# Gate and local input of a two-layer adaLN kernel: unrolled, three batches in flight, slots cleared inside the gate

## The reference, cut to what matters

```python
h = _layernorm(x) * (1 + ca) + sa
x = x + ga * attention(h)
h = _layernorm(x) * (1 + cb) + sb
x = x + gb * ffn(h)
```

## Time and profile before

| | us |
|---|---|
| median of three runs | 2258.83 |
| the profiled execution | 2267.06 |
| its span, first to last instruction | 2265.3 |
| mean granted clock of TensorE | 0.864 |

### The profile page before, as it was taken

The page is one execution under the profiler, slowest core; times in us unless marked ns, Lnnn a source line. Parts: engine busy times, 40 slices in busy tenths (PEclk is TensorE's granted clock), DMA queues, the critical chain, the costliest instruction groups (busy, mean ns, idle before and its releaser), DMA issues. The chain is left out here.

```text
span 2265.3 us, 41710 instructions
## 1 busy us (share of the span) xinstructions
PE 1832.3 (81%) x13060; PEld 956.2 (42%) x13060; DVE 1412.9 (62%) x2467; ACT 1164.9 (51%) x2814; POOL 932.5 (41%) x1035
## 2 busy tenths in 40 slices
PE   4798899875439247999999995569999999999996
PEld 2344444433328132333333322435555555555552
DVE  4566566642402325777677781368788888888872
ACT  0265455550014012766566673047677777777772
POOL 3255445441230520222222111157667666666660
PEclk9699899985569555999899997579999999999996
DMA  2122222222124311222222221311111111111110
GB/s 69 53 85 80 76 85 76 80 77 85 35 61 116 113 37 63 71 86 80 84 96 86 85 72 61 125 27 31 37 45 36 34 37 41 52 40 41 38 54 18
DMA packets 93887, 145.35 MB, mean 64 GB/s; under 512 B 13544, under 2 KB 46507, under 8 KB 93480
## 3 DMA queue, kind: packets, MB, share of 16 engines
q1 hardware_dynamic: 91688, 139.33, 19.5%
q0 software_dynamic: 2048, 4.16, 0.7%
HBM read 78.74 MB, written 49.28 MB: 57 GB/s over the span
## 5 line engine op out<-in xcount | busy, mean ns | idle before, releaser
L1152 DVE TENSOR_REDUCE M_sb<-banks 128x1 f32<-128x512 f32 (+3 forms) x1024 | 549.8, 581 | 297.2 <-PE banks L756 148.8
L948 ACT ACTIVATE probs_sb<-banks 128x512 f32<-128x512 f32 (+3 forms) x1024 | 474.8, 516 | 327.6 <-PE banks L788 322.3
L753 PE MATMUL banks<-K_sb,Q_sb 72*128 72x512 bf16 (+3 forms) x1024 | 377.8, 374 | 48.4 <-issue 21.0
L788 PE MATMUL banks<-Q_sb,K_sb 75*128 75x512 bf16 (+3 forms) x1024 | 362.3, 361 | 34.7 <-DMA Q_sb<-mrows_sb 27.8
L804 PE MATMUL banks<-probs_sb,V_sb 128*32 128x512 f32 (+3 forms) x2048 | 253.1, 561 | 6.5 <-POOL probs_sb L1041 5.2
L753 PEld LDWEIGHTS banks<-K_sb,Q_sb 72*128 72x128 bf16 x1024 | 105.6, 103 | 316.9 <-DVE M_sb L1152 162.3
L2150 ACT ACTIVATE l_p_sb<-banks,l_nb_sb,l_inv_sb 128x128 f32<-128x128 f32 x512 | 228.4, 466 | 10.2 <-DVE l_nb_sb L2322 9.4
L2228 POOL TENSOR_TENSOR l_inv_sb<-l_clip_sb,l_minus_half_sb 128x16 f32<-128x16 f32 x64 | 186.3, 2911 | 55.8 <-DVE l_clip_sb L2297 54.0
L2236 POOL TENSOR_TENSOR l_pn_sb<-l_p_sb,l_rs_sb 128x512 f32<-128x512 f32 x128 | 150.3, 1174 | 143.3 <-DVE l_rs_sb L2328 141.8
L2221 POOL TENSOR_TENSOR l_ts_sb<-l_t_sb 128x1024 f32<-128x1024 f32 x64 | 153.3, 2396 | 43.3 <-DVE l_t_sb L2276 26.2
L788 PEld LDWEIGHTS banks<-Q_sb,K_sb 75*128 75x128 bf16 x1024 | 103.6, 102 | 135.2 <-ACT probs_sb L948 36.2
(11 more groups left out here) (247 smaller groups left out, 3491.9 us busy)
## 6 DMA issues: line engine op xcount, KB each, us to landing
Q_sb<-qk_dram SPq DMA_DIRECT2D x192, 96.0 KB
o_dram<-osum_sb SPq DMA_DIRECT2D x64, 256.0 KB, 2.8
l_vs_sb<-l_vt_sb SPq DMA_DIRECT2D x112, 128.0 KB, 2.3
qk_dram<-parts_sb SPq DMA_DIRECT2D x96, 128.0 KB
K_sb<-qk_dram SPq DMA_DIRECT2D x32, 288.0 KB
x_norm_sb<-x SPq DMA_DIRECT2D x24, 256.0 KB, 2.8
spack_sb<-o_dram SPq DMA_DIRECT2D x16, 256.0 KB, 3.6
opack_sb<-o_dram SPq DMA_DIRECT2D x16, 256.0 KB, 3.7
```

Of the source, the lines that this page charges most:

```text
L753: mm = pe.matmul(out[:, 0:width], g.Q[0:RK, par, q, h, k * P:(k + 1) * P], g.K[0:RK, par, qk(q), hk(h), 0:width], start=True, stop=not causal)
L788: pe.matmul(SB[ring % 3][:, t0:N], g.K[0:RM, slot, qk(q), hk(h), k * P:(k + 1) * P], g.Q[0:RM, slot, q, h, t0:N], start=True, stop=True).t ...
L948: act.activation(g.probs[:, k, h, t0:N], SB[ring % 3][:, t0:N], ACT.Exp, scale=scale)\
L1152: dve.reduce_max(g.M[:, u % 2, k, h:h + 1], SA[ring % 3][:, 0:width], AX.X, negate=True)\
```

## The change

The gate and the local input get helpers of their own (`stream_*`), which take constants for the batch: all eight batches are written out, with no hardware loop. x has four buffers, the centred x three, its square two, h two. Mean uses banks 0 and 1 in turn, variance bank 2, spread banks 3 and 4 in turn, transposes bank 5, logits bank 6. In step n PE does the mean of batch n, the variance of n-1, the spread of n-2, and in the gate the transposes and logits of n-3. The Block that cleared the slots is gone; a transfer at the end of SP's program in the gate writes them from one row of zeros, which POOL sets in the first Block of the kernel. Two DVE multiplications by 1.0 become copies. The attention's waits for loads are counted anew, with no other difference.

```diff
@@ load_constants, POOL
                 pool.memset(g.zero[:, :], 0.0)
+                pool.memset(g.zero_row[:, :], 0.0)
                 pool.memset(g.V[:, :, :, :, :], 0.0).then_inc(padded, 1)
...
+def allocate_stream(g):
+    g.sx = g.sb("s_x", [P, XS, N])
+    g.sxc = g.sb("s_xc", [P, 3, N])
+    g.ssq = g.sb("s_sq", [P, 2, N])
+    g.sh = g.sb("s_h", [P, 2, N])
+
+def stream_load(g, sp, base, it, x):
+    if it >= XS:
+        sp.wait_ge(g.ns["xc"], base + it - XS + 1)
+    sp.dma_start(g.sx[:, it % XS, :], x[it]).then_inc(g.ns[f"x_loaded{it % XS}"], 16)
+
+def stream_mean(g, pe, base, it, done):
+    s, slot = g.ns, it % XS
+    pe.wait_ge(s[f"x_loaded{slot}"], ((done if slot < FIRST else done // 2) + it // XS + 1) * 16)
+    pe.wait_ge(s["xc"], base + it - 1)
+    pe.matmul(g.bank[it % 2][:, :], g.mean_w[:, :], g.sx[:, slot, :], start=True, stop=True).then_inc(s["mean"], 1)
+
+def stream_variance(g, pe, base, it):
+    s = g.ns
+    pe.wait_ge(s["sq"], base + it + 1)
+    pe.wait_ge(s["veps"], base + it)
...
+def stream_spread(g, pe, base, it):
+    s = g.ns
+    pe.wait_ge(s["spread"], base + it + 1)
+    pe.wait_ge(s["xh"], base + it - 1)
...
+def stream_finish(g, dve, base, it, col, reader, count):
+    s = g.ns
+    dve.wait_ge(s["rstd_psum"], base + it + 1)
+    dve.wait_ge(s["h"], base + it)
+    dve.tensor_tensor(g.xh[:, :], g.sxc[:, it % 3, :], g.bank[3 + it % 2][:, :], ALU.mult).then_inc(s["xh"], 1)
+    dve.wait_ge(s["xh"], base + it + 1)
+    if it >= 2:
+        dve.wait_ge(reader, count)
...
@@ setup_experts
-    with nc.Block() as block:
-        @block.gpsimd
-        def _(pool):
-            pool.memset(g.htok[:, :, :], 0.0).then_inc(s["zeros"], 1)
-
-        @block.sync
-        def _(sp):
-            sp.wait_ge(s["zeros"], 1)
-            rows = g.slots.rearrange("(p r) c -> p r c", p=P)
...
-            sp.wait_ge(s["zeroed"], 32)
+    allocate_stream(g)
@@ gate
+            for it in range(XS):
+                stream_load(g, sp, base, it, x)
             sp.dma_start(g.wg[:, :], g.ins["wg"]).then_inc(s["setup"], 16)
             sp.dma_start(g.route_c[:, :], g.ins["route_c"]).then_inc(s["setup"], 16)
-            for slot in range(2):
-                norm_load(g, sp, base + slot, slot, x[slot])
-            paired(sp, 0, B, batch)
+            for it in range(XS, B):
+                stream_load(g, sp, base, it, x)
+            sp.dma_start(g.slots.rearrange("(p r) c -> p r c", p=P),
+                         g.zero_row[:, :].unsqueeze(1).broadcast_to([P, E * CAP // P, C])).then_inc(s["zeroed"], 16)
+            sp.wait_ge(s["zeroed"], 16)
...
+            for n in range(B + 3):
+                if n < B:
+                    stream_mean(g, pe, base, n, 1)
+                if 1 <= n <= B:
+                    stream_variance(g, pe, base, n - 1)
+                if 2 <= n <= B + 1:
+                    stream_spread(g, pe, base, n - 2)
+                if n >= 3:
+                    if n == 3:
+                        pe.wait_ge(s["setup"], 32)
+                    turn(n - 3)
...
+            for n in range(B + 3):
+                if 2 <= n <= B + 1:
+                    norm_repeat(g, dve, base + n - 2)
+                if n < B:
+                    stream_center(g, dve, base, n)
+                if 1 <= n <= B:
+                    stream_epsilon(g, dve, base, n - 1)
+                if 2 <= n <= B + 1:
+                    stream_finish(g, dve, base, n - 2, n - 2, s["lpsum"], n - 3)
+                if n >= 3:
+                    keep(n - 3)
@@ local_input (PE and DVE in the same order, without turn and keep), SP
+                for it in range(B + 2):
+                    if it < B:
+                        stream_load(g, sp, base, it, x)
+                    if it >= XS:
+                        n = it - XS
+                        sp.wait_ge(g.ns["h"], base + n + 1)
+                        sp.dma_start(h_out[n], g.sh[:, n % 2, :]).then_inc(stored[n % 2], 16)
+                for n in range(B + 2 - XS, B):
+                    sp.wait_ge(g.ns["h"], base + n + 1)
+                    sp.dma_start(h_out[n], g.sh[:, n % 2, :]).then_inc(stored[n % 2], 16)
```

More of the change, by code:

```diff
@@ L31 @@
 FIRST = 2
+XS = 4
 PAIRS, HD = 4, 64
@@ new lines, in stream_square, with stream_center @@
+def stream_square(g, act, base, it):
+    s = g.ns
+    act.wait_ge(s["xc"], base + it + 1)
+    act.wait_ge(s["var"], base + it - 1)
+    act.activation(g.ssq[:, it % 2, :], g.sxc[:, it % 3, :], ACT.Square).then_inc(s["sq"], 1)
+def stream_center(g, dve, base, it):
+    s = g.ns
+    dve.wait_ge(s["mean"], base + it + 1)
+    dve.wait_ge(s["sq"], base + it - 2)
+    dve.wait_ge(s["xh"], base + it - 2)
+    dve.tensor_tensor(g.sxc[:, it % 3, :], g.sx[:, it % XS, :], g.bank[it % 2][:, :], ALU.subtract)\
+       .then_inc(s["xc"], 1)
@@ L1318, in _, with turn @@
-            paired(sp, 0, B, batch)
+            for it in range(XS, B):
[3 more added lines that the diff above has]
+            sp.wait_ge(s["zeroed"], 16)
         @block.tensor
         def _(pe):
[L1322 to L1329, removed]
+            def turn(it):
+                pe.wait_ge(g.ns["h"], base + it + 1)
+                if it:
+                    pe.wait_ge(s["htok"], it)
@@ L1344, in _ @@
         @block.scalar
         def _(act):
[L1346 to L1351, removed]
+            for it in range(B):
+                stream_square(g, act, base, it)
         @block.gpsimd
         def _(pool):
-            def batch(it, slot, last):
-                norm_power(g, pool, it + base)
-            paired(pool, 0, B, batch)
+            for it in range(B):
+                norm_power(g, pool, base + it)
@@ L1360, in _, with keep @@
         @block.vector
         def _(dve):
[L1362 to L1372, removed]
+            def keep(it):
+                at = slice(it * CH, (it + 1) * CH)
@@ L1380, in _ @@
-            norm_center(g, dve, base, 0)
-            norm_epsilon(g, dve, base)
-            paired(dve, 0, B, batch)
+                dve.tensor_copy(g.logits[:, at, :], g.bank[6][:, 0:CH * E].rearrange("p (c n) -> p c n", c=CH))\
+                   .then_inc(s["logits"], 1)
+            for n in range(B + 3):
[9 more added lines that the diff above has]
+                    keep(n - 3)
@@ new lines, in local_input, with _ @@
+    with g.memory():
+        allocate_stream(g)
+        with nc.Block() as block:
+            @block.sync
+            def _(sp):
+                for it in range(B + 2):
[8 more added lines that the diff above has]
+                    sp.dma_start(h_out[n], g.sh[:, n % 2, :]).then_inc(stored[n % 2], 16)
+                for half in stored:
+                    sp.wait_ge(half, B // 2 * 16)
+            @block.tensor
+            def _(pe):
+                for n in range(B + 2):
+                    if n < B:
+                        stream_mean(g, pe, base, n, 4)
+                    if 1 <= n <= B:
+                        stream_variance(g, pe, base, n - 1)
+                    if n >= 2:
+                        stream_spread(g, pe, base, n - 2)
+            @block.scalar
+            def _(act):
+                for it in range(B):
+                    stream_square(g, act, base, it)
+            @block.gpsimd
+            def _(pool):
+                for it in range(B):
+                    norm_power(g, pool, base + it)
+            @block.vector
+            def _(dve):
+                for n in range(B + 2):
+                    if n >= 2:
+                        norm_repeat(g, dve, base + n - 2)
+                    if n < B:
+                        stream_center(g, dve, base, n)
+                    if 1 <= n <= B:
+                        stream_epsilon(g, dve, base, n - 1)
+                    if n >= 2:
+                        stream_finish(g, dve, base, n - 2, n - 2 + B, stored[n % 2], (n - 2) // 2 * 16)
```

106 lines of the change are left out of this document (31 added, 75 removed).

## The result

The kernel after takes 2208.06 us (median of four runs, 2206.93 to 2211.97), the kernel before 2259.85 (median of four, 2257.73 to 2266.81): 51.8 us less by the medians, whose quotient is 0.977. The ratio on record is lower, 0.974 with a 95% interval of 0.9715 to 0.9765, which would be 53 to 64 us less; it agrees with 2208.06 against the highest of the four runs of before. The prediction said 2226 with a range of 2205 to 2241 and 33 us less; the gain is half as large again by the medians, three quarters by the ratio.

A forecast was written before the change was run, and what follows sets the result against it. The prediction took PE, at a mostly slow clock, to fill the gate and local input, each alone on the span. 14 + 19 = 33 us off the profiled 2267.06 gave 2234, or 2226 as median; range 2205 to 2241.

The forecast's parts named there:

- I take the gate to run at 1.2 GHz but for one stretch: Gate: mean, variance, spread, transposes, logits (M, V, S, T, L) take 7.75 us a batch at the slow clock.
- Being busy is not enough: Gate: PE 4.34 of 5.00 us busy stayed at clock 0.50, so busyness alone was held not to raise it.
- the cases that the range was drawn for: Whole kernel: the forecast (chance 0.61) and both stages at 1.2 GHz (2236.5 us, chance 0.18).
- rival 2: Gate and local input both at 2.4 GHz from the first batches: 63.9 us less, 2195; chance 0.12.
- Clearing block: Ahead of the gate: the block clearing the slots leaves the path, first load issued 12.7 us earlier.
- the four loads' interleaving: Gate's start: four loads at once might land x[0] up to 1.6 us later; taken as 0.
- Clearing transfer: End of SP's gate program: 2.62 MB of zeros, done by 573 before the block ends, so it costs nothing.
- Rival 4: Clearing transfer sets the gate's end if over 48 us; slower than before if over 81 us; chance 0.03.
- Gate's batches: Gate: waits removed, PE work unchanged, mostly 1.2 GHz with one fast stretch; 14 us less including the clearing.
- Local input: Local input: first four batches slow at 5.3 us, the rest fast at 3.0; 19 us less.
- Unrolled code: Both stages: fetching straight code taken as 0 of 0 to 17.6 us; as a rival 2243 us, chance 0.06.
- The sum: Whole kernel: 14 for gate and clearing plus 19 for the local input, 33 us less.

The follow-up runs named there:

- own_bank: Kernel after's gate with the old one-batch local input, whose variance alone gets its own bank, against the kernel before: 2226.84 us, ratio 0.983.
- idle: Kernel after with four extra DVE copies in each gate step from step 4 on, PE's program unchanged: 2223.49 us, 0.9817 of before.
- fill_joined: Kernel after with four 8-column matmuls ahead of the spread in gate steps 1 and 3: 2212.82 us, 0.9767 of before.
- fill_parted: Kernel after with four 8-column matmuls ahead of the mean in gate steps 1 and 3: 2215.87 us, and 2217.25 when run again.
- warm: joined with two 512-column matmuls at the start of both stages and one in each step without a mean: 2198.71 us, 0.9692 of before.
- unroll: Kernel before with the gate's and local input's loops written out, nothing else: 2265.17 us, 0.9977 of before.
- joined: Kernel after with the gate's spread last in each step, next to the following mean: 2213.21 us, 0.9759 of before.
- warm_columns: warm with each stage's two opening matmuls replaced by two groups of four one-column matmuls: 2203.66 us, 0.9729 of before.

## Why the prediction was too cautious

The step that failed is this one: "V stands between M and S, T and L between S and the next M ... I take the gate to run at 1.2 GHz but for one stretch". Instead the gate ran at 1.00 for 20.5 of its 48.05 us, at 3.98 a batch and not 7.75. Two things were wrong in the step.

- *The filling.* Step 2 has no transposes and logits yet, so spread 0 and mean 3 do stand side by side, and in after the clock rises there. Step 0 has only a mean, so means 0 and 1 stand side by side too, and in own_bank's gate it rises behind them. I wrote down the steady order and did not write out the first four steps.
- *What lets the clock fall.* In the earlier trace rows it fell behind V, T and L with PE 2.13 of 3.00 busy. I put the fall on their kind; after and idle show the same kinds, between means and spreads, holding 1.00 until PE has a gap. The kind is not without weight either: in fill_joined the clock fell with PE 3.30 of 3.30 busy. "Being busy is not enough" was right for a rise (fill_parted, 43.30 us), but the row it was drawn from, 4.34 of 5.00 busy, has a gap and could not show it.

That 2208.06 lies in the range at all is luck: the cases that the range was drawn for have the gate at 1.00 for one stretch at most.

The Trainium skill, "TensorE: Matmul & The Clock Gate", section "Why this matters for your kernels", which the prediction weighed as rival 2, gives the full clock to an engine kept continuously busy. By that row the gate comes out nearer; the 43.30 us of fill_parted contradict it for the rise. For holding, the 20.5 us of after agree, and the 3.30 us of fill_joined do not.

Step by step:

- *Clearing block*, 12.7 less: 12.66 in the profile, 7.7 (3 to 13) alone by medians. From the first load to the first mean, where the four loads' interleaving was put at 0 of 0 to 1.6, it took 513.52 - 510.23 = 3.29 instead of 2.76: 0.5 more. It is not the interleaving: the local input's four loads took 1361.23 - 1358.46 = 2.77, and before's gate, with two, 533.18 - 530.19 = 2.99.
- *Clearing transfer*: forecast to leave at 533.7 and to be done by 573, that is 16.2 and at most 55.5 behind the first load; it left at 527.06, 16.8 behind it, and had landed 28.8 behind it. Rival 4 needed over 48 us; it took 11.3.
- *Gate's batches*: forecast 14 less with the clearing, rival 2 37.4, measured 30.5. Its steady period was 4.2 in rival 2, by DVE; 3.98 was measured, PE's own sum of 4.0, and DVE was busy for 15.03 of 20.50 us. What it lacks of 37.4 is the ends: 12.68 us of PE work ahead of the rise and 10.41 behind the fall ran at 0.50, and rival 2 had only 4.5 for filling and draining. Own_bank's execution of the same gate, which has all but the first 6.8 us at 1.00, is 7.6 below after's (48.05 - 40.47): 38.1 less with the clearing, against rival 2's 37.4.
- *Local input*: the mechanism was right, slow and then fast, 19 less. Measured 22.7: the rise came at mean 3 instead of after four batches, a fast batch took 2.85 instead of 3.0. In six other profiles with the same local input (without warm's matmuls) it took 34.3 to 38.8; after's, at 38.8, is at the slow end of them, and the size of the gain hangs on the execution.
- *Unrolled code*, 0 of 0 to 17.6: 0, by unroll. The page that the prediction named, the Trainium skill's "Advanced Engine Details and Errata", section "ISA Cache", has the cache hold few lines of 256 instructions, from which the prediction inferred that straight code must be fetched; no cost of it shows in these two stages.
- *The sum*: 33, measured 51.8. Of the missing 19, 16.5 is the gate's clock (30.5 - 14) and 3.7 the local input's, less 1.5 elsewhere. Rival 2, at 63.9, is 12.1 off on the other side: right for the middle of both stages, wrong for their ends.

## What to carry to other kernels

Where the clock alternates, ask two questions and not one: what raises it, and what lets it fall again. The steady batch held 1.00 here as long as PE had no gap, and lost it in idle when PE got one; but other mixes fell without a gap. So write out the first steps of a pipeline instruction by instruction, and read the clock in the profile. Matmuls of 512 columns before the first data arrive and where the engine's own run out are worth a trial: with them the kernel took 14.5 us less than joined. A deeper pipeline is worth more than the wait it removes if it also keeps the engine fed at the higher clock: own_bank got 9.0 of 22.6 us. And when one profile is compared with another, look first whether the same program repeats its time: this gate took 40.47, 48.05 and 48.29 us in three.

## What the runs showed that I had not expected

- One order of instructions with no idle time ran at either clock for long: 7.68 us a batch in fill_parted, which stayed at 0.50 for 43 us, 3.98 in after, which stayed at 1.00 for 20.
- A clock at 1.00 fell with PE 3.30 of 3.30 us busy (fill_joined), and in another execution held with PE 7.16 of 10.00 busy (own_bank's gate).
- 3.30 us of one-column matmuls at full occupancy (PEld 3.30 too) left the clock at 0.50 in warm_columns; 3.02 us of 512-column ones stood ahead of a rise in warm, while 3.78 us of them in after (513.52 on) did not.
- The 2.62 MB of zeros, read from one row per partition in pieces of 512 B, landed in 11.3 us behind the last load of x, 232 GB/s, against 6.4 us for the 2 MB of the earlier trace rows.
- Kernels that differ only in these two stages spread by 10 us in attention 0 (its last store between 507.8 and 518.0), so a gain below that can't be read from one profile's total.
